# Second attention's scores without block-diagonal keys, and TensorE matmuls whose results nobody reads

## The chip, the cores and the metric

The kernel runs on one core of a Trainium2 chip. The metric is the device time of one execution in microseconds, of which several executions give a median. TensorE (PE) multiplies matrices, VectorE (DVE), ScalarE (ACT) and GpSimd (POOL) work on rows of up to 128 partitions, and SyncE (SP) issues transfers (DMAs). Each engine runs its own list of instructions in order; semaphores join them.

## The reference, cut to what matters

```python
x = x + window_attention(group_norm(x))     # 16 images of 16x16 tokens, 128 channels; 16 heads of 32
t = to_tokens(x)
t = t + attn(ln(t))                         # the second attention: 8 heads of 16
t = t + moe(ln(t))                          # 8 experts, top 2 of them for each token

def attn(x):                                # one image: 256 tokens, 128 channels
    qkv = x @ w_qkv + b_qkv
    q, k, v = heads_of_16(qkv)
    attn = softmax(einsum('bhqd,bhkd->bhqk', q, k) * c ** -0.5)
    return einsum('bhqk,bhkd->bhqd', attn, v) @ w_out + b_out
```

The second attention's scores are, for each of the 8 heads, a product of 256 queries and 256 keys over 16 channels. The kernel splits queries and keys into a high part rounded to the type fp32r and the remainder as a low part, and sums the four products of the parts.

## The kernel before, in words

All 16 images are software-pipelined. An iteration i works on up to eight images at once, each in another stage, and each engine goes through eight steps n = 0 to 7 in an order written out by hand. The stages are X (group norm, image i+2), G (queries, keys and values of the first attention, i+1), A (windowed first attention, i), M (its output projection, layer norm, and the projections of the second attention, i-1), Bm (the second attention, one head per step n, i-2), R (its output projection, i-3), L (router logits; the image's `slots` in DRAM are cleared, i-4) and K (each token's place in its experts' lists, and four indirect scatters of token rows on GpSimd at n = 6, i-5). Iterations 0 to 1 are the ramp, 16 to 20 the drain. An image's period here runs from one head 0 of Bm to the next. Four periods come before the first scatters; the ten after them hold scatters, and then the drain begins. After the drain the routing tables are finished, 39 tiles of 256 rows go through the experts (L1365 to L1393), and the two rows of each token are added.

The second attention before the change: at n = 5 of M, ScalarE writes the keys' high part (L646) and VectorE the low part (L929) into `kst1`. SyncE waits for the low part (`m_klo`) and copies the 16 rows of each head with one DMA into `kbd1` (L433, eight for an image). `kbd1` holds four blocks of 256 columns for each of two groups of heads, a head's block being zero outside its 16 rows, so that a matmul over all 128 rows of `q1` sees one head alone. GpSimd clears the two buffers once (L505). At n = 6 ScalarE (L675) and VectorE (L903) write `q1` likewise. In an iteration's step n, head n of Bm takes four matmuls with 256 moving columns (L1180), which at n = 0 wait for the queries' low part and for the eight DMAs (L1174), and on every odd step for the first attention's adds. They write `pSB` on even and `pSA` on odd steps. Then, at n = 0 and n = 4, come the windowed scores of A in 32x64 tiles (L1199) into `pSA` and `pTA`. VectorE takes the rows' maxima (L938), ScalarE the exponentials (L704), VectorE the reciprocals of their sums (L838), GpSimd multiplies (L548), and two steps later TensorE transposes (L1211); four heads at a time it multiplies by the values (L1227, 128x32 tiles). GpSimd's list also holds the first attention's multiply (L556) in front of the transposes L1296, and the scatters (L582).

SyncE's list for an iteration is: the next image's tokens `xt` (L413), the 1 MB of zeros into `slots` (L419), the residual (L424), which waits for R at n = 5, and the eight key copies (L433). Split products are three matmuls each, L1139 to L1141; L1286 is the first attention's output projection.

## Time and profile before

| | us |
|---|---|
| median of 3 runs | 817.3 |
| lowest, highest | 813.43, 821.74 |
| the profiled execution's own time | 815.25 |
| its span in the profile | 813.4 |
| mean granted TensorE clock over the span | 0.899 |

The durations used are those of the profiled execution, so a sum over them stands against 815.25 us, which is 2.05 us below the median of the three runs; the span leaves 1.85 us outside it. A granted clock of 1.00 is 2.4 GHz, one of 0.50 is 1.2 GHz; a mean between them says how much of a stretch stood at either.

### The profile page before, as it was taken

Reading aid. Unit: us, or ns where it says so; the run is one execution under the profiler, and the core shown is the slowest. Engines: PE = TensorE matmul, PEld = TensorE weight load, DVE = VectorE, ACT = ScalarE, POOL = GpSimd, SP = SyncE. Lnnn points to the kernel's source line nnn. Section 1 sums busy time; section 2 is a strip of 40 time slices with the busy share of each in tenths; the row PEclk is TensorE's granted clock in tenths of the full one; section 3 lists DMA queues with packets and bytes.
Section 4 is the critical chain, followed back from the end, with each engine's and each line's share of the span. In section 5 each row is a group of like instructions: output and inputs, shape, how many; then the busy total and the mean of one; then the engine's idle time right before and its main releaser. Section 6 shows DMA issues by size and latency. Waiting matters only on the chain. (4 is left out here: it accounts for less than half of the span.)

```text
span 813.4 us, 19815 instructions
## 1 busy us (share of the span) xinstructions
PE 636.2 (78%) x6838; PEld 536.7 (66%) x6838; DVE 513.5 (63%) x1513; ACT 509.5 (63%) x1427; POOL 479.3 (59%) x556
## 2 busy tenths in 40 slices
PE   2777898998999988898888998878753299998920
PEld 2556787776777767677777777756542187887810
DVE  5665767777778687777867778674332355564522
ACT  3555878787777688777877777655540166665600
POOL 6354556557675766867667575674554335655645
PEclk9698999999999899999999999897785599999965
DMA  7002203123041321404314041230732212222248
GB/s 206 14 2 34 32 5 93 21 75 90 18 107 19 89 49 59 105 9 100 60 48 103 12 99 27 81 81 25 197 126 78 66 54 79 83 83 68 79 120 219
DMA packets 54218, 59.25 MB, mean 73 GB/s; under 512 B 10371, under 2 KB 49411, under 8 KB 53603
## 3 DMA queue, kind: packets, MB, share of 16 engines
q1 hardware_dynamic: 44918, 45.65, 22.3%
q0 software_dynamic: 4544, 9.38, 3.2%
q10 hardware_dynamic: 4656, 2.95, 1.3%
q8 instruction: 56, 0.92, 0.5%
q14 instruction: 44, 0.35, 0.1%
HBM read 36.00 MB, written 28.64 MB: 79 GB/s over the span
## 5 line engine op out<-in xcount | busy, mean ns | idle before, releaser
L548 POOL TENSOR_TENSOR pb<-pb,rcb 128x512 f32<-128x512 f32 x128 | 155.5, 1215 | 177.2 <-DVE rcb L838 176.5
L593 POOL DMA_INDIRECT ysl<-yo,dst x78 | 74.7, 957 | 68.6 <-issue 33.5
L704 ACT ACTIVATE pb<-pSB,mxb 128x256 f32<-128x256 f32 x128 | 59.5, 469 | 58.9 <-DVE mxb L938 58.4
L1211 PE MATMUL pTB<-ident,pb 128*128 128x128 f32 x512 | 86.5, 296 | 12.1 <-ACT ptb L718 8.0
L556 POOL TENSOR_TENSOR pa<-pa,rca 128x512 f32<-128x512 f32 x64 | 67.2, 1051 | 29.0 <-DVE rca L1003 29.0
L718 ACT ACTIVATE ptb<-pTB 128x512 f32<-128x512 f32 x128 | 77.0, 602 | 6.0 <-PE pTB L1211 5.2
L704 ACT ACTIVATE pb<-pSA,mxb 128x256 f32<-128x256 f32 x128 | 59.7, 475 | 32.2 <-DVE mxb L938 25.8
L582 POOL DMA_INDIRECT slots<-rec,slot x64 | 63.2, 988 | 18.5 <-issue 17.2
L1211 PEld LDWEIGHTS pTB<-ident,pb 128*128 128x128 f32 x512 | 62.9, 150 | 16.5 <-issue 10.7
L938 DVE TENSOR_REDUCE mxb<-pSB 128x2 f32<-128x512 f32 x64 | 43.9, 686 | 41.4 <-PE pSB L1180 21.5
L724 ACT ACTIVATE pta<-pTA 128x512 f32<-128x512 f32 x64 | 38.4, 599 | 44.3 <-PE pTA L1296 44.1
L1180 PE MATMUL pSB<-kbd,q 128*128 128x256 f32 x256 | 47.6, 310 | 13.4 <-issue 11.6
L1296 PE MATMUL pTA<-ident,pa 128*128 128x128 f32 x256 | 43.6, 298 | 14.0 <-POOL pa L556 8.3
L1086 DVE COPY xs<-pG 128x256 f32<-128x256 f32 x39 | 16.6, 425 | 59.0 <-PE pG L1365 33.6
L1180 PEld LDWEIGHTS pSB<-kbd,q 128*128 128x128 f32 x256 | 37.5, 200 | 21.7 <-issue 19.3
L1139 PE MATMUL pG<-xnh,w0h 128*128 128x256 f32 x120 | 42.8, 357 | 11.2 <-POOL xnl L570 5.5
L1180 PE MATMUL pSA<-kbd,q 128*128 128x256 f32 x256 | 50.9, 325 | 0.0
L938 DVE TENSOR_REDUCE mxb<-pSA 128x2 f32<-128x512 f32 x64 | 43.9, 686 | 10.7 <-PE pSA L1180 9.6
L1271 PE MATMUL pOA<-pta,v 128*64 128x64 f32 x1024 | 45.9, 234 | 6.1 <-ACT t2f L686 3.6
L993 DVE TENSOR_REDUCE sma<-pa 128x8 f32<-128x512 f32 x64 | 43.6, 681 | 10.9 <-ACT pa L694 10.3
L1199 PE MATMUL pTA<-k,q 32*64 32x64 f32 x1024 | 43.6, 229 | 8.6 <-issue 8.6
L1271 PEld LDWEIGHTS pOA<-pta,v 128*64 128x64 f32 x1024 | 37.3, 143 | 17.8 <-issue 13.7
(213 smaller groups left out, 1955.3 us busy)
## 6 DMA issues: line engine op xcount, KB each, us to landing
slots<-sel_dram SPq DMA_DIRECT2D x16, 1040.0 KB
kbd<-kst SPq DMA_DIRECT2D x128, 64.0 KB
xt<-slots SPq DMA_DIRECT2D x39, 130.0 KB
xch<-x_ch_dram SPq DMA_DIRECT2D x4, 512.0 KB, 6.8
xt<-x_tok_dram SPq DMA_DIRECT2D x16, 128.0 KB
xch<-t SPq DMA_DIRECT2D x16, 128.0 KB, 2.0
fw<-f_dram SPq DMA_DIRECT2D x1, 2048.0 KB, 9.1
yc<-ysl SPq DMA_DIRECT2D x8, 256.0 KB, 9.3
```

Of the source, the lines that this page charges most:

```text
L548: pool.tensor_tensor(pb[:, b, :, :], pb[:, b, :, :], rcb[:, b, :].unsqueeze(2).to_broadcast([128, 2, TOK]), ALU.mult).then_inc(sb_nrm, 1)
L556: pool.tensor_tensor(pa[:, u, :, :], pa[:, u, :, :], rca[:, b, :].unsqueeze(2).to_broadcast([128, 8, WIN]), ALU.mult).then_inc(sa_nrm, 1)
L582: pool.indirect_dma_start(slots, bass.IndirectOffsetOnAxis(ap=slot[:, K.par, k, s:s + 1], axis=0), rec[:, K.par, s, k, :], None).then_inc( ...
L593: pool.indirect_dma_start(ysl, bass.IndirectOffsetOnAxis(ap=dst[:, t % YB, n:n + 1], axis=0), yo[:, t % YB, n, :], None).then_inc(y_dma[t ...
L704: last = a.activation(pb[:, b, qc, :], (pSB, pSA)[n % 2][:, qc * TOK:(qc + 1) * TOK], ACT.Exp, bias=mxb[:, b, qc:qc + 1], accum_out=smb[:, ...
L718: a.activation(ptb[:, (J.j * BU + k) % PTBUFS, :, :], pTB[:, :].rearrange("p (a b) -> p a b", a=2), ACT.Copy).then_inc(tb_ev, 1)
L938: v.tensor_reduce(mxb[:, b1, :], bank[:, :].rearrange("p (a k) -> p a k", a=2), AX.X, ALU.max, negate=True).then_inc(sb_max, 1)
L993: v.tensor_reduce(sma[:, b, :], pa[:, u, :, :], AX.X, ALU.add).then_inc(sa_sum, 1)
L1180: mm = pe.matmul((pSB, pSA)[n % 2][:, qc * TOK:(qc + 1) * TOK], q1[:, Bm.par, n // 4, qc * 128:(qc + 1) * 128], kbd1[Bm.par][:, part, n // ...
L1199: mm = pe.matmul(bank[WIN * w:WIN * w + WIN, (pr * NCH + c) * WIN:(pr * NCH + c + 1) * WIN], q0[D0 * r:D0 * r + D0, A.par, c, t:t + WIN], ...
L1211: mm = pe.transpose(pTB[:, kc * TOK + qc * 128:kc * TOK + (qc + 1) * 128], pb[:, k % PBUFS, qc, kc * 128:(kc + 1) * 128], ident[:, :])
L1271: mm = pe.matmul(pOA[WIN * jj:WIN * jj + WIN, w * WIN:(w + 1) * WIN], v0[:, J.par, w, jj, u, :, :].rearrange("p a d -> p (a d)"), pta[:, u ...
```

## The change

Keys: `kst1`, `kbd1`, the eight DMAs of each image (128 in all), the two clears and the waits on them are gone. The columns of the second attention's query and key weights are permuted on the chip into `w1p`, so that the 16 channels that the weights held for the high part of a head and the 16 for its low part come out in 32 adjacent rows. Queries: ScalarE multiplies by `is_low`, which is 0 or 1 for each row, with a bias `bq1l` to match; VectorE's part now spans 128 rows and not 64. Keys are written straight into `k1` and read from there. A head's four matmuls read rows 32*(n % 4) to 32*(n % 4) + 31 of `q1` and `k1`; their number and their 256 columns are as before.

Setup: the biases `bq1` and `bk1` are loaded with 16 small DMAs where there were 2, ahead of `bv1s`, `rws` and `rbs` on SyncE; ScalarE has four strided copies of 128 x 128 and one of 256 columns where it had one scaling of 256 columns; VectorE gets two small operations.

Unread matmuls: `keep_awake(bank, count)` issues matmuls of 128x128 by 512 columns of `w0h` into a bank that is free at that point. There are 6 ahead of the first image's projections; 1 a step in iteration 1; 3 (`AWAKE`) ahead of the scores of steps 0 and 4 in each of 14 iterations, behind waits for VectorE's adds and ScalarE's evictions that free `pTA`, waits which before stood only behind the head's own scores; 12 and 2 ahead of transposes of image 0; 2 a step in iterations 15 (but step 0) and 16; and 4 a step in 17 and 18. Another 32, of 128 columns in full fp32, stand between the last product of the routing tables and the experts' first tile.

```diff
-            sp.dma_start(bq1s[:, :], bq1).then_inc(d_c1, 16)
-            sp.dma_start(bk1s[:, :], bk1).then_inc(d_c1, 16)
+            for r in range(4):
+                for t in range(2):
+                    rows, of_head = slice(PAD1 * r + D1 * t, PAD1 * r + D1 * t + D1), slice(64 * t + D1 * r, 64 * t + D1 * r + D1)
+                    sp.dma_start(bq1s[rows, :], bq1[of_head, :]).then_inc(d_c1, 16)
+                    sp.dma_start(bk1s[rows, :], bk1[of_head, :]).then_inc(d_c1, 16)
...
-                    for h in range(8):
-                        rows = slice(D1 * h, D1 * h + D1)
-                        sp.dma_start(kbd1[M.par][rows, :, :, h % 4, :].bitcast(f32), kst1[rows, :, :, :].bitcast(f32))\
-                          .then_inc(k1_dma[M.par], 16)
...
-                        wait(a, k1_dma[(M.par + 1) % 2],
-                             (M.half + M.par) * 128 if M.j > 0 else 0)
+                        wait(a, sb_mm, (M.j - 1) * BU)
...
                             last = a.activation(q1[:, M.par, g, :], pM[:, g * TOK:(g + 1) * TOK], ACT.Identity,
-                                                bias=bq1x[:, g:g + 1])
+                                                scale=is_low[:, 0:1], bias=bq1l[:, g:g + 1])
...
-                    a.activation(w1s[:, 0:QK1], w1s[:, 0:QK1], ACT.Copy, scale=SCALE1).then_inc(c_w1s, 1)
+                    for k in range(2):
+                        for t in range(2):
+                            a.activation(w1p[:, k * QK1:(k + 1) * QK1].rearrange("p (g r t d) -> p g r t d", g=2, t=2, d=D1)
+                                         [:, :, :, t, :],
+                                         w1s[:, k * QK1:(k + 1) * QK1].rearrange("p (g t r d) -> p g t r d", g=2, t=2, d=D1)
+                                         [:, :, t, :, :], ACT.Copy, scale=(SCALE1, 1.0)[k])
+                    a.activation(w1p[:, 2 * QK1:], w1s[:, 2 * QK1:], ACT.Copy).then_inc(c_w1s, 1)
...
+            def keep_awake(bank, count):
+
+                for _ in range(count):
+                    pe.matmul(bank[:, :], w0h[:, 0:128], w0h[:, 0:512], start=True, stop=True)
...
+                    if A is not None and M is not None and Bm is None:
+                        keep_awake(pSB, 1)
+                    if Bm is not None and A is not None and n % 4 == 0:
+                        wait(pe, sa_add, A.j * AU + n // 2)
+                        wait(pe, ta_ev, A.j * AU + n // 2 - 1)
+                        keep_awake(pTA, AWAKE)
+                    if G is None and Bm is not None and M is not None:
+                        if n > 0 or A is None:
+                            pe.wait_ge(g_ev, B * GU)
+                            keep_awake(pG, 2)
+                    elif A is None and R is not None:
+                        keep_awake(pG, 4)
                     if Bm is not None:
...
-                            pe.wait_ge(k1_dma[Bm.par], Bm.half * 128 + 128)
...
+                        r, g = PAD1 * (n % 4), n // 4
                         for qc in range(2):
                             for part in range(2):
                                 mm = pe.matmul((pSB, pSA)[n % 2][:, qc * TOK:(qc + 1) * TOK],
-                                               q1[:, Bm.par, n // 4, qc * 128:(qc + 1) * 128],
-                                               kbd1[Bm.par][:, part, n // 4, n % 4, :],
+                                               q1[r:r + PAD1, Bm.par, g, qc * 128:(qc + 1) * 128],
+                                               k1[r:r + PAD1, Bm.par, part, g, :],
                                                start=(part == 0), stop=(part == 1))
...
+            for _ in range(GATHER_AWAKE):
+                pe.matmul(pOB[:, 0:128], ones[:, :], later[:, :], start=True, stop=True)
             turn_tokens(0)
```

SyncE's instructions in two steady iterations, before: each iteration's key copies stand between its residual (`xch<-t2`) and the next tokens.

```order
L413 DMA xt<-x_tok_dram 128x2x128
L419 DMA slots<-sel_dram 8x4x8320
L424 DMA xch<-t2 128x256
L433 DMA kbd1_0<-kst1 16x4x256 x8
L413 DMA xt<-x_tok_dram 128x2x128
L419 DMA slots<-sel_dram 8x4x8320
L424 DMA xch<-t2 128x256
```

The same of the changed kernel: the next tokens and the zeros follow the residual directly, so they are issued as soon as that is, and no longer behind the wait for the keys' low part.

```order
L419 DMA xt<-x_tok_dram 128x2x128
L425 DMA slots<-sel_dram 8x4x8320
L430 DMA xch<-t2 128x256
L419 DMA xt<-x_tok_dram 128x2x128
L425 DMA slots<-sel_dram 8x4x8320
L430 DMA xch<-t2 128x256
L419 DMA xt<-x_tok_dram 128x2x128
```

TensorE from the end of an iteration's step 7 to the first tiles of A in the next, before: the value product of G, head 0's scores, then A.

```order
L1211 MATMUL pTB<-ident,pb 128x128 x4
L1271 MATMUL pOA<-pta,v0 64x64 x8
L1139 MATMUL pG<-wvh,xnh 128x512
L1140 MATMUL pG<-wvh,xnl 128x512
L1141 MATMUL pG<-wvl,xnh 128x512
L1180 MATMUL pSB<-kbd1_0,q1 128x256 x4
L1199 MATMUL pSA<-k0,q0 64x64 x2
L1199 MATMUL pTA<-k0,q0 64x64 x2
```

The same of the changed kernel: three unread matmuls into `pTA` have come in ahead of head 0's scores, which read `k1`.

```order
L1295 MATMUL pOA<-pta,v0 64x64 x8
L1143 MATMUL pG<-wvh,xnh 128x512
L1144 MATMUL pG<-wvh,xnl 128x512
L1145 MATMUL pG<-wvl,xnh 128x512
L1151 MATMUL pTA<-w0h 128x512 x3
L1204 MATMUL pSB<-k1,q1 128x256 x4
L1223 MATMUL pSA<-k0,q0 64x64 x2
L1223 MATMUL pTA<-k0,q0 64x64 x2
```

TensorE at the end of the drain, before: the last output projection, router logits and places, the last product of the routing tables (`total`), and the experts' first transposes (`xt2`).

```order
L1350 MATMUL pM<-ahead,ones 128x16
L1227 MATMUL pOB<-ptb,v1 32x256 x8
L1242 MATMUL pOA<-wo1s,o1 128x128 x4
L1310 MATMUL pOA<-ident,tn2 128x128 x2
L1336 MATMUL pM<-rws,t2f 128x8 x2
L1348 MATMUL pM<-both,later 128x16
L1350 MATMUL pM<-ahead,ones 128x16
L1348 MATMUL pM<-both,later 128x16
L1350 MATMUL pM<-ahead,ones 128x16
L1358 MATMUL pM<-total,ones 128x8
L1365 MATMUL pG<-ident,xt2 128x128 x2
```

The same of the changed kernel: unread matmuls between the steps' short products, and 32 behind the product of `total`.

```order
L1266 MATMUL pOA<-wo1s,o1 128x128 x4
L1151 MATMUL pG<-w0h 128x512 x8
L1336 MATMUL pOA<-ident,tn2 128x128 x2
L1151 MATMUL pG<-w0h 128x512 x4
L1362 MATMUL pM<-rws,t2f 128x8 x2
L1374 MATMUL pM<-both,later 128x16
L1376 MATMUL pM<-ahead,ones 128x16
L1374 MATMUL pM<-both,later 128x16
L1376 MATMUL pM<-ahead,ones 128x16
L1384 MATMUL pM<-total,ones 128x8
L1423 MATMUL pOB<-later,ones 128x128 x32
L1391 MATMUL pG<-ident,xt2 128x128 x2
```

## Rows read from the trace of the kernel before

**Rows 1.** The page: busy time and share of the engines.
```profile
PE 636.2 (78%) x6838; PEld 536.7 (66%) x6838; DVE 513.5 (63%) x1513; ACT 509.5 (63%) x1427; POOL 479.3 (59%) x556
```

**Rows 2.** The waits: engine line waited for: us in all, times, longest.
```profile
POOL pb L548 <- DVE rcb L838: 176.5, 102, 5.6
PE pSB L1180 <- issue: 11.6, 14, 3.0
```

**Rows 3.** Windows: length, busy us (x) of PE, PEld, DVE, ACT, POOL, clock, DMA.
```profile
134.00:166.00 32.00, 28.48 (x384) 24.13 (x384) 25.30 (x68) 25.23 (x78) 17.83 (x20) 1.00 0.20 50
305.00:339.00 34.00, 28.91 (x388) 24.70 (x389) 26.23 (x74) 26.38 (x80) 23.72 (x29) 1.00 0.27 70
198.33:545.56 347.23, 302.95 (x3850) 258.11 (x3851) 261.75 (x738) 257.18 (x773) 232.85 (x275) 0.95 0.25 63
551.00:562.00 11.00, 11.00 (x73) 8.95 (x72) 2.33 (x10) 4.45 (x14) 3.54 (x5) 0.54 0.03 8
578.10:591.70 13.60, 10.97 (x57) 9.14 (x57) 3.65 (x14) 5.97 (x19) 7.03 (x10) 0.50 0.94 283
```

**Rows 4.** The timeline of TensorE: back-to-back matmuls.
```profile
213.64 0.28 PE L1141 MATMUL pG<-xnl,w0h 128*128 128x256 f32 x1
213.76 0.38 PE L1211 MATMUL pTB<-ident,pb 128*128 128x128 f32 x2
...
286.38 0.39 PE L1140 MATMUL pG<-wvh,xnl 128*128 128x512 f32 x1
286.61 0.39 PE L1141 MATMUL pG<-wvl,xnh 128*128 128x512 f32 x1
...
297.05 0.28 PE L1141 MATMUL pG<-xnl,w0h 128*128 128x256 f32 x1
297.26 0.42 PE L1227 MATMUL pOB<-ptb,v 128*32 128x256 f32 x4
```

**Rows 5.** The timeline of an image with scatters, by engine.
```profile
297.09 5.10 SPq L433 DMA_DIRECT2D kbd<-kst  x8
...
304.87 0.70 PE L1180 MATMUL pSB<-kbd,q 128*128 128x256 f32 x4 [0.88 <-issue]
...
307.20 0.69 DVE L938 TENSOR_REDUCE mxb<-pSB 128x2 f32<-128x512 f32 x1 [2.67 <-remote]
...
305.39 0.96 POOL L582 DMA_INDIRECT slots<-rec,slot  x1 [0.30 <-issue]
...
307.37 1.04 POOL L556 TENSOR_TENSOR pa<-pa,rca 128x512 f32<-128x512 f32 x1
```

**Rows 6.** The timeline of TensorE: head 0 of the first and the fourth image.
```profile
71.40 0.71 PE L1180 MATMUL pSB<-kbd,q 128*128 128x256 f32 x4 [1.79 <-DMA kbd<-kst]
...
166.32 0.72 PE L1180 MATMUL pSB<-kbd,q 128*128 128x256 f32 x4 [0.63 <-issue]
```

**Rows 7.** The setup: SyncE and ScalarE.
```profile
2.16 6.39 SPq L388 DMA_DIRECT2D posr<-pos_dram  x16
...
18.00 0.43 SPq L405 DMA_DIRECT2D rbs<-rb_dram  x1
...
22.49 0.42 ACT L730 ACTIVATE q<-q 128x256 f32<-128x256 f32 x1 [0.29 <-DMA rbs<-rb_dram]
```

**Rows 8.** The chain that ended last, 540 to 660 us: start, us, what.
```profile
558.70 3.12 PE pM L1286 x16
577.00 3.02 issue
...
646.65 2.05 PE pSA L1372 x4
...
654.10 0.86 PE pSA L1372 x4
```

**Rows 9.** The timeline of TensorE: a warm out-projection, the first expert tile.
```profile
487.72 2.05 PE L1286 MATMUL pM<-wo0s,o 128*128 128x128 f32 x16
...
645.28 0.69 PE L1365 MATMUL pG<-ident,xt 128*128 128x128 f32 x2 [9.58 <-DMA xt<-slots]
```

46 lines of the change are left out of this document (27 added, 19 removed).

## The prediction

> **What bounds the kernel now.** I read the page's shares first, then the waits, then windows of single images, then the timeline around head 0, and last the chain that ended last. No engine is full: PE is the busiest with 78% of the span [rows 1]. In an image without scatters PE is busy for 28.5 of 32.0 us, in one with scatters for 28.9 of 34.0 us, at the full clock in both [rows 3]. So a steady image is some 29 us of PE work and 3.5 to 5 us of gaps, while GpSimd has slack: most of its idle time goes to waits for VectorE's reciprocals [rows 2]. PE's order, with the loop scores, maximum, exponential, reciprocal, multiply, transposes laid over it, sets the period, and what is added to PE lands on the path unless it falls into one of these gaps.
>
> Two places in a period are not PE's work. At head 0 PE stands for the key copies: SyncE needs 5.10 us to issue the eight of them [rows 5], and the idle time before the head's first matmul was 1.79 us in the first image and 0.63 us in the fourth [rows 6]; over the four periods without scatters the four of them sum to 5.2 us. In an image with scatters PE waited 0.88 us for it, and the head's scores, begun at 304.87, reached VectorE only at 307.20, after 2.67 us idle [rows 5]; without scatters the four matmuls take 0.72 us [rows 6]. So some 1.6 us more go there, with the key copies and the scatters (last one at 305.39) in flight together.
>
> The drain is another thing: there PE stood 3.02 us for the last image's copies, and its clock is low: 0.54 in 551 to 562 us and 0.50 in 578 to 592 us [rows 3, 8]. The same 16 matmuls take 3.12 us there and 2.05 us warm [rows 8, 9].
>
> **The change, part by part.** The sum is made against the profiled execution's 815.25 us, 2.05 us under the median of the runs shown.
>
> *Setup.* SyncE gets 14 more DMAs ahead of `rbs`. Sixteen small ones took 6.39 us, 0.40 each [rows 7], so `rbs` comes 5.6 us later; ScalarE's first scaling waits for exactly that DMA [rows 7] and everything in its list stands behind it, then VectorE's low part and the projections of image 0. Then ScalarE has five copies instead of one of 0.42 us: four of half the columns and one like it, some 1.5 us instead of 0.42, so +1.1. Together +6.7. The two clears of `kbd1` leave GpSimd's list, which has time then. The unread matmuls of the ramp keep the clock up for image 0's steps; I take 1.2 us for that (bounds 0 and 2.5), an estimate from what one fall costs below. **Ramp +5.5.**
>
> *Scores in 32 rows.* The count and the 256 columns are the same, so the matmuls cost the same; the trace has no 32-row matmul with 128 stationary columns, so I bound what surrounds it. A full-array product followed by another starts 0.12 us after it, followed by a 128x32-tile product 0.21 us after it [rows 4]: 0.09 us for going into another tile shape, and I take the same for coming out. Six heads pay both, the two that A's tiles follow only one: 6 x 0.18 + 2 x 0.09 = 1.26 us an image. Bounds: 0 (if rows alone are not such a shape) and 2.5 (if each costs double). The Trainium skill, in TensorEngine Tiling (Array Packing), on tiling modes, says that a change of mode drains the array; the rows agree that a change costs something, and the sum by either is this one.
>
> *Unread matmuls in the steady state.* 512 columns take 0.23 us at the full clock [rows 4]: six an image are 1.38 us. With the switches that is 2.64 us. PE's gaps (3.5 us an image [rows 3]) hide a part, mainly at step 4, where the evictions of the value product are waited for: I count 2.3 on the path. The waits ahead of them are for things that A's tiles two places on wait for anyway; behind them are head 0's and head 4's scores, and through these VectorE's maximum. Bounds: 0 and 2.64.
>
> *Four periods without scatters:* 4 x 2.3 = 9.2, less the 5.2 us of key waits. **+4.0.**
>
> *Ten periods with scatters:* of the 2.64 us, 0.78 (three unread matmuls and one switch) stand at step 0, where the stall was; the rest is 1.86, of which I take 1.3 on the path. At step 0, without the 0.88 us and the 1.6 us, GpSimd is next: after the last scatter (305.39) come two multiplies, the second of which, for A, starts at 307.37 and takes 1.04 us [rows 5], and step 1's transposes of `pa` need it. The step can come at most 1.0 us sooner. Net +0.3 an image. **+3.** The earlier `xt` and zeros on SyncE (they no longer queue behind the key copies) go to buffers that are waited for an image later, and take no time; if the 1 MB now meets the scatters, that is the second rival.
>
> *Clock in the steady state.* 198.33 to 545.56 us are ten periods at a mean clock of 0.95 [rows 3], that is 34 us at 1.2 GHz. Ten undisturbed ones would be 340 us, so the falls cost 7.2 us. They begin just after step 0, where PE stands idle and then runs A's 32x64 tiles. The change removes the idle time and puts three full-array products there, but makes eight sets of scores narrow. I take three quarters of it back, **-5.4** (bounds -7.2 and +9).
>
> *Drain.* The wait of 3.02 us goes, but for the queries' low part and the switch: -2.5. At 1.2 GHz PE pieces take half as long again [rows 8, 9]; the two windows of 11.0 and 13.6 us hold 22 us of busy PE [rows 3], a third of which is 7.3; the unread matmuls should save most, less what they add themselves to the short steps: -6. The first expert tile has 2.05 us where later ones have 0.86 [rows 8], and 32 unread matmuls stand ahead of it: -1.5. They are full fp32 of 128 columns; eight such products are the 16 pieces of 2.05 us warm or 3.12 us cold [rows 8, 9], so 32 are 8.2 to 12.5 us, where PE idled 9.58 us before the tile's first transposes [rows 9]. If the clock doesn't rise in them, they end 3 us late. **-10** (bounds -13 and +1).
>
> The sum: 5.5 + 4.0 + 3.0 - 5.4 - 10.0 = -2.9, which is 812.3 us.
>
> **The rivals.**
> 1. *PE isn't what binds.* If switches and unread matmuls fall into gaps, two thirds of the 9.2 + 13 us counted for them vanish: about 797 us. For it: 3.5 to 5 us of gaps in every period [rows 3]. Against: the gaps are waits inside the loop, and a later matmul moves them along.
> 2. *The stall at step 0 stays.* The label on VectorE's wait names no releaser [rows 5], so the key copies need not be the cause: GpSimd's scatters with the zeros and tokens that now come earlier would do as well. Then the 1.0 us of ten periods is not gained: 812 + 10 = 822 us. The zeros may then also hold up the scatters by themselves.
> 3. *The clock falls more often,* the slower side. In 551 to 562 us PE was busy for the whole 11.00 us at a clock of 0.54, and in 134 to 166 us for 89% of it at 1.00 [rows 3], so it isn't busy time that keeps the clock, but what is done. If scores of 32 rows keep it up worse than those of 128, and six unread matmuls an image don't make up for it, the falls double: +7.2 in place of -5.4, and 4 us of the drain's gain go: 829 us. It decides from about fourteen falls in the steady state, where there are eight stretches now.
> 4. *Weight loads come into the open.* All four matmuls of a head now use the same 32 rows. If each load then waits for the matmul ahead of it, that is at least one more spacing of 0.12 us for each [rows 4], 32 an image: 3.8 x 15 = 58 us, about 870 us. Against it: products that use the same (all) rows follow each other after 0.12 us with a load between them [rows 4]. The Trainium skill, in TensorE: Matmul & The Clock Gate, Part 3, says that loads overlap matmuls in flight only when the row group differs; by that rule this rival would happen, and before's rows speak against it.
>
> **How the numbers follow.** The forecast (0.44) is 812 us, by itself 802 to 820. Rival 1 has 0.20, rival 2 0.21, rival 3 0.12, rival 4 0.03. The range 797 to 829 leaves out half of rivals 1 and 3 and all of 4, a little under two in ten. A measurement can tell about 1%, here 809.1 to 825.5. Faster by over 1%: 0.17 of the forecast, 0.19 of rival 1: 0.36. Slower: 0.08 of rival 2, 0.10 of rival 3, and rival 4: 0.21. Within: 0.43.
>
> **What would show it.** After the change, head 0's first row should have no idle time from keys; VectorE's maximum at step 0 should wait under 1 us in a period with scatters, with GpSimd running from the first scatter to A's multiply without idle (else rival 2). Full-array products should start 0.09 us later next to scores than before (rivals 1 and 4: nothing, or 0.12 more per matmul). The windows of ten periods should have a clock of 0.98 or more (rival 3: 0.91). A's first tiles should come 5 to 6 us later, and the last product of head 7's drain some 8 us nearer to the start of its image. The prediction would be most wrong if the ramp's 14 DMAs were hidden, or the clock went the other way.

## The result

The changed kernel takes 871.28 us (median of 4 runs, 864.54 to 873.86) against 818.16 us for the kernel before beside it (median of 4): a ratio of 1.061 (1.057 to 1.066), slower. The profiled execution's span is 862.7 us against 813.4 us. The forecast was 812 us, within 797 to 829.

Head 0 of Bm marks the periods in both traces. The first scatters' period begins at 198.3 us before and 201.4 us after; the fifteenth image's head 0 comes at 545.6 and 608.9 us; the ends are the spans. So the 49.3 us come from three pieces:

| | before | after | difference | forecast |
|---|---|---|---|---|
| start to the first period with scatters | 198.3 | 201.4 | +3.1 | +9.5 |
| the ten periods with scatters | 347.2 | 407.5 | +60.3 | -2.4 |
| from there to the end | 267.8 | 253.8 | -14.0 | -10.0 |

Head 0 stands in the spans, so these are pieces of the two profiled executions, of which the changed kernel's was the fastest of its four. What made the change slower lies in the ten periods.

The page of the changed kernel, first the engines' shares, as in [rows 1], then the granted clock of TensorE in 40 slices:

```profile
PE 740.3 (86%) x7112; PEld 598.8 (69%) x7112; DVE 503.7 (58%) x1515; ACT 516.8 (60%) x1431; POOL 472.1 (55%) x554
...
PEclk9799999999969696979788887978999789999975
```

PE is busier by 104 us, though only some 57 us of unread matmuls were added (210 of 512 columns at 0.23 us and the 32, 9 us): the same instructions last longer. The clock row shows 6 to 8 in most slices from the twelfth to the twenty-eighth, where the periods with scatters lie. The waits, as in [rows 2]:

```profile
POOL pb L541 <- DVE rcb L836: 230.1, 96, 6.5
...
DVE mxb L936 <- remote: 25.3, 9, 2.8
```

GpSimd waits longer for the reciprocals, since the whole loop is longer; and VectorE's wait for head 0, labelled remote, is still there (nine times, up to 2.8 us), though the key copies are gone. The wait of PE for key copies is no longer among its rows. Windows, columns as in [rows 3]: one period without scatters, one with, and the ten together:

```profile
134.50:167.70 33.20, 31.32 (x392) 25.54 (x391) 25.15 (x69) 26.47 (x80) 18.64 (x21) 1.00 0.11 42
319.60:360.60 41.00, 38.00 (x395) 30.89 (x394) 25.57 (x74) 26.81 (x79) 23.64 (x29) 0.83 0.11 41
201.40:608.90 407.50, 378.52 (x3924) 303.80 (x3923) 255.29 (x737) 262.65 (x775) 234.14 (x276) 0.84 0.11 41
```

Without scatters the period is 33.2 us where it was 32.0 [rows 3], at the full clock. With them it is 41.0 us at a mean of 0.83, and eight periods in a row are 41.0 to 41.2 us. In all but the first of the ten a low stretch begins some 4 us after head 0 and lasts 13.65 us; the tenth has another of 6.8 us, and the first only one of 3.4 us. One period, cut at the two places (columns as above, the clock third from the end): ahead of the fall TensorE is busy for 3.04 of 4.10 us, in it for 13.18 of 13.65.

```profile
360.63:364.73 4.10, 3.04 (x76) 2.75 (x75) 1.50 (x3) 3.09 (x10) 3.77 (x6) 1.00 0.12 37
364.73:378.38 13.65, 13.18 (x75) 10.29 (x74) 6.05 (x18) 6.17 (x19) 7.43 (x10) 0.50 0.00 1
378.38:401.61 23.23, 21.81 (x248) 17.85 (x247) 18.02 (x54) 17.55 (x52) 12.46 (x14) 1.00 0.17 65
```

TensorE's timeline at the end of that fall, and at the next head 0:

```profile
372.19 1.22 PE L1204 MATMUL pSB<-k,q 32*128 32x256 f32 x4
...
376.88 2.77 PE L1310 MATMUL pM<-wo0s,o 128*128 128x128 f32 x16
379.50 0.60 PE L1322 MATMUL pTA<-ident,pa 128*128 128x128 f32 x4
380.03 0.74 PE L1204 MATMUL pSA<-k,q 32*128 32x256 f32 x4
380.70 0.39 PE L1143 MATMUL pG<-xnh,w0h 128*128 128x256 f32 x1
...
400.84 0.84 PE L1151 MATMUL pTA<-w0h 128*128 128x512 f32 x3
401.61 0.73 PE L1204 MATMUL pSB<-k,q 32*128 32x256 f32 x4
```

The four scores of head 2 (372.19) last 1.22 us, the out-projection 2.77 us where 2.05 is warm [rows 9], and behind it everything is back: the scores at 380.03 take 0.74 us. So the clock rises in the out-projection that follows head 2, and not before it. The last two rows show the price of the three unread matmuls (0.77 us from the first of them to the scores, at the full clock) and that the four narrow scores take 0.73 us, where four over 128 rows took 0.70 to 0.72 [rows 5, 6]: their weight loads are as hidden as before. GpSimd and VectorE around the same head 0:

```profile
398.41 1.07 POOL L575 DMA_INDIRECT slots<-rec,slot  x1 [0.17 <-issue]
...
402.31 0.96 POOL L575 DMA_INDIRECT slots<-rec,slot  x1 [0.30 <-issue]
...
404.29 1.06 POOL L549 TENSOR_TENSOR pa<-pa,rca 128x512 f32<-128x512 f32 x1
...
404.16 0.69 DVE L936 TENSOR_REDUCE mxb<-pSB 128x2 f32<-128x512 f32 x1 [2.82 <-remote]
```

The scores' rows end at 401.61 + 0.73 = 402.34, but VectorE can read them only at 404.16, 1.8 us later. This is the stall of [rows 5], 2.82 us idle where it was 2.67, with no key copy in flight.

### The profile page after: what moved, and what is told of

Read it like the earlier page. It is cut to its first block and busy times, and to the rows that moved or that the text cites. A ratio compares the mean times of both kernels' runs of the same rounds, so it can differ in the third digit from the quotient of the medians.

```text
span 862.7 us, 20278 instructions
## 1 busy us (share of the span) xinstructions
PE 740.3 (86%) x7112; PEld 598.8 (69%) x7112; DVE 503.7 (58%) x1515; ACT 516.8 (60%) x1431; POOL 472.1 (55%) x554
## 5 line engine op out<-in xcount | busy, mean ns | idle before, releaser
L1235 PE MATMUL pTB<-ident,pb 128*128 128x128 f32 x512 | 90.2, 304 | 4.4 <-ACT ptb L710 2.5
L716 ACT ACTIVATE pta<-pTA 128x512 f32<-128x512 f32 x64 | 38.2, 597 | 77.0 <-PE pTA L1322 77.0
L1143 PE MATMUL pG<-xnh,w0h 128*128 128x256 f32 x120 | 48.7, 406 | 4.9 <-ACT v L655 2.8
L1204 PE MATMUL pSB<-k,q 32*128 32x256 f32 x256 | 51.7, 325 | 0.0
L1204 PE MATMUL pSA<-k,q 32*128 32x256 f32 x256 | 51.6, 324 | 0.0
L1295 PE MATMUL pOA<-pta,v 128*64 128x64 f32 x1024 | 48.2, 242 | 2.6 <-ACT pta L716 1.1
L1295 PEld LDWEIGHTS pOA<-pta,v 128*64 128x64 f32 x1024 | 39.4, 150 | 15.0 <-issue 11.3
L1223 PE MATMUL pSA<-k,q 32*64 32x64 f32 x1024 | 41.0, 222 | 10.0 <-issue 10.0
L1204 PEld LDWEIGHTS pSB<-k,q 32*128 32x128 f32 x256 | 37.8, 204 | 15.6 <-issue 14.2
L1204 PEld LDWEIGHTS pSA<-k,q 32*128 32x128 f32 x256 | 37.6, 203 | 15.1 <-issue 15.1
L747 ACT ACTIVATE ws<-fw 128x773 f32 x39 | 33.0, 848 | 25.0 <-DVE t_exp L1052 18.2
```

Source lines behind the costliest of these rows:

```text
L1143: pe.matmul(out_, wh, xh, start=True, stop=False)
L1204: mm = pe.matmul((pSB, pSA)[n % 2][:, qc * TOK:(qc + 1) * TOK], q1[r:r + PAD1, Bm.par, g, qc * 128:(qc + 1) * 128], k1[r:r + PAD1, Bm.par, ...
L1235: mm = pe.transpose(pTB[:, kc * TOK + qc * 128:kc * TOK + (qc + 1) * 128], pb[:, k % PBUFS, qc, kc * 128:(kc + 1) * 128], ident[:, :])
L1295: mm = pe.matmul(pOA[WIN * jj:WIN * jj + WIN, w * WIN:(w + 1) * WIN], v0[:, J.par, w, jj, u, :, :].rearrange("p a d -> p (a d)"), pta[:, u ...
```

## The experiments

The runs came to four chips, each time with the kernel before beside them, and the ratios are against that. First chip (kernel before 794 us): e1 to e4. Second (822 us): c1, c2, e5, e6. Third (821 to 823 us): c3, e7, e8, e9, e14, e15. Fourth (828 us): e10 to e13. Times of different chips are not compared, only ratios and what the periods look like. In the last column are the ten periods from the fifth head 0 to the fifteenth, with their mean clock, in the profiled execution. Other numbers in the scores (e1, e5, e7, e12, e14, e15) mean that the kernel no longer computes the reference; its instructions stay the same.

| | edit | median us | ratio (95%) | ten periods: us, clock |
|---|---|---|---|---|
| e1 | scores over 128 rows, first chip | 794.6 | 1.000 (0.997 to 1.003) | 339.3, 0.97 |
| e2 | scatters behind the pipeline | 866.4 | 1.090 (1.081 to 1.098) | 346.0, 0.97 |
| e3 | no steady unread matmuls | 834.6 | 1.050 (1.043 to 1.058) | 384.7, 0.85 |
| e4 | before, with the unread matmuls of the ends | 785.8 | 0.990 (0.983 to 0.997) | 336.0, 0.97 |
| c1 | the changed kernel, second chip | 869.5 | 1.061 (1.055 to 1.068) | 407.5, 0.84 |
| c2 | the kernel before, second chip | 822.3 | 1.000 (0.996 to 1.003) | 355.1, 0.92 |
| e5 | scores over 64 rows | 865.0 | 1.057 (1.051 to 1.063) | 406.6, 0.84 |
| e6 | 12 unread matmuls for 3 | 879.1 | 1.073 (1.067 to 1.080) | 396.6, 0.94 |
| e7 | scores over 128 rows, third chip | 808.0 | 0.983 (0.977 to 0.989) | 351.8, 0.96 |
| c3 | the changed kernel, third chip | 866.5 | 1.053 (1.045 to 1.060) | 405.0, 0.84 |
| e8 | scatters at step 7 | 842.9 | 1.023 (1.018 to 1.029) | 375.5, 0.94 |
| e9 | as e4, third chip | 811.8 | 0.987 (0.981 to 0.993) | 349.5, 0.95 |
| e10 | 1 unread at each step | 878.6 | 1.065 (1.055 to 1.076) | 402.2, 0.86 |
| e11 | 2 unread at each step | 917.9 | 1.105 (1.090 to 1.119) | 434.6, 0.82 |
| e12 | two bias DMAs | 881.1 | 1.063 (1.053 to 1.073) | 412.1, 0.83 |
| e13 | e4 and the scatters at step 7 | 832.8 | 1.005 (1.000 to 1.009) | 368.0, 0.93 |
| e14 | 128 rows at steps 0 to 2 | 814.5 | 0.992 (0.988 to 0.996) | 354.6, 0.96 |
| e15 | 128 rows at steps 3 to 7 | 846.3 | 1.033 (1.024 to 1.041) | 375.6, 0.90 |

### The width of the scores: e1, e7, c3, e5

```diff
-                                               q1[r:r + PAD1, Bm.par, g, qc * 128:(qc + 1) * 128],
-                                               k1[r:r + PAD1, Bm.par, part, g, :],
+                                               q1[:, Bm.par, g, qc * 128:(qc + 1) * 128],
+                                               k1[:, Bm.par, part, g, :],
```

> The changed kernel with one difference: the second attention's scores read all 128 rows of q1 and k1 in place of a head's 32, so a score is the sum over four heads (the softmax and all behind it computes on other numbers). Count, columns, waits and unread matmuls are those of the changed kernel. After the change a period with scatters takes 41.0 us with 13.65 us of it at half clock. Theory A (the narrow scores are what lets the clock fall): periods of 34 to 35 us, mean clock over the ten periods at least 0.97, time 800 to 812 us. Theory B (the stall during the scatters, not the width of the scores, lets the clock fall): periods stay near 41 us, time 865 to 875 us. Theory C (leaving and entering narrow tiles costs): periods some 1.2 us shorter, clock as it is.

The ten periods were 33.4 to 35.0 us, and the ratio 1.000, as theory A (the narrow scores let the clock fall) has it. But this first chip had something else: head 0 came without the stall. TensorE's and VectorE's rows of e1 in a period with scatters:

```profile
231.42 0.63 PE L1204 MATMUL pSB<-k,q 128*128 128x256 f32 x4
...
232.08 0.69 DVE L936 TENSOR_REDUCE mxb<-pSB 128x2 f32<-128x512 f32 x1 [0.80 <-PE pSB L1204]
```

The scores end at 231.42 + 0.63 = 232.05 and VectorE reads at 232.08. So e1 had neither the narrow scores nor the stall, and it could not tell which of the two absences mattered. The changed kernel had to be seen again, and e1 repeated where the stall is.

> The changed kernel itself once more, since the kernel before took 794 us here against 817 us where it was first compared, and TensorE's lag during the scatters (1.6 to 2.3 us a period there, before and after) was absent in the profiles of the first four experiments. Theory A (narrow scores let the clock fall, whatever the stall): periods with scatters of 38 to 41 us, ratio 1.05 to 1.07. Theory B (the stall tips it): without the stall no falls, periods of 34 us, ratio 0.98 to 1.00.

> The kernel before itself once more, for a profile beside the others. No lag during the scatters, periods with scatters of some 33.5 us against 34.8 where it was first profiled, ratio 1.00.

This second chip had the stall in both kernels, against what I had expected of c2, and the kernel before had periods of 34.6 to 37.1 us; c1 repeats the 41.0 us and the 1.061. It left the question where it was, so both went to a third chip together:

> The changed kernel with scores over all 128 rows again (a sum over four heads; the softmax and all behind it computes on other numbers), because the first time it ran where TensorE shows no lag during the scatters, and the changed kernel itself was seen only where it does (periods of 41.0 us, ratio 1.061; with 64 rows the same). If the width alone decides: periods of 34 to 36 us and a ratio of 0.97 to 1.01 with the lag too. If the lag alone decides: 41 us and 1.06 with the lag, wherever the scores are read from.

> The changed kernel beside it. With the lag during the scatters: 41.0 us a period and 1.061, as twice. Without the lag: if the width alone decides, 38 to 41 us and 1.05 or more; if lag and width are both needed, 34 us and 0.98 to 1.00.

That chip has the stall: in nine of c3's ten periods and in six of e7's, VectorE reads head 0's scores 1.7 to 2.2 us after their end. Windows of e7: a stretch as long as a period, with scatters and at the full clock, and the ten periods:

```profile
230.00:264.00 34.00, 30.09 (x394) 25.93 (x394) 25.66 (x75) 26.47 (x79) 23.50 (x28) 1.00 0.13 49
196.10:547.90 351.80, 314.18 (x3924) 271.42 (x3923) 259.46 (x737) 259.75 (x774) 232.39 (x274) 0.96 0.13 47
```

The same ten of c3, beside it on the chip:

```profile
206.10:611.10 405.00, 376.74 (x3925) 301.94 (x3924) 255.19 (x737) 263.07 (x775) 232.58 (x274) 0.84 0.11 41
```

The same instructions (3924 and 3925 matmuls), waits, unread matmuls and scatters take 351.8 us over 128 rows and 405.0 us over 32; the whole kernel 808.0 and 866.5 us. With the stall present in both, the width alone decides: theory A. That e7 computes on other numbers doesn't explain it, since e5 below does so too and keeps the falls. In e7 the falls last 3.4 us each and come in seven of the ten periods.

> The changed kernel with scores read from 64 rows of q1 and k1 (two heads summed; the softmax and all behind it computes on other numbers). Theory A, by how much of the array a score fills: between 32 rows and 128 rows, so falls in some periods with scatters, periods of 34 to 38 us, 800 to 835 us. If only the tile mode mattered, it would be as the changed kernel with 32 rows.

My expectation was wrong: 64 rows are no middle. Eight of its ten periods are 40.9 to 41.2 us with 13.65 us at half clock, as with 32 rows.

### Which scores: e14, e15

```diff
+                        rows = slice(0, 128) if n < 3 else slice(r, r + PAD1)      # e14;  e15: n > 2
...
-                                               q1[r:r + PAD1, Bm.par, g, qc * 128:(qc + 1) * 128],
-                                               k1[r:r + PAD1, Bm.par, part, g, :],
+                                               q1[rows, Bm.par, g, qc * 128:(qc + 1) * 128],
+                                               k1[rows, Bm.par, part, g, :],
```

> The changed kernel with scores over all 128 rows at steps 0, 1 and 2 and narrow ones at steps 3 to 7 (the heads of the wide steps are sums over four heads; all behind computes on other numbers). If the heads in the thin stretch keep the clock down: falls of 3.4 us or none, 34 to 36 us a period, 0.98 to 1.01. If it is the period as a whole: 37 to 41 us.

> The reverse: narrow at steps 0, 1 and 2, all 128 rows at steps 3 to 7 (again other numbers). If the thin stretch decides: 40 to 41 us a period with 13.65 us at half clock, 1.05 to 1.06. If the period as a whole does: 35 to 38 us, since five of eight heads are wide.

The ten periods of e14, and then of e15:

```profile
199.90:554.50 354.60, 328.09 (x3924) 271.27 (x3923) 258.62 (x737) 261.11 (x774) 232.52 (x274) 0.96 0.13 46
```

```profile
204.10:579.70 375.60, 340.87 (x3924) 286.68 (x3923) 257.64 (x737) 260.29 (x775) 231.51 (x274) 0.90 0.12 44
```

Both ran on the chip of e7 and c3. Three wide heads of eight bring 405.0 us to 354.6, the five others bring it to 375.6 only. In e14 a period has 3.4 us at half clock, once 6.8 and twice none; in e15 four have 13.65 to 17.1 us (40.1 to 42.3 us a period) and three none (33.6 to 34.1 us). So no long fall came with wide heads at steps 0 to 2. Narrow ones there bring them, but not in every period as long as the other five are wide: of the six falls behind head 0 in e15 four last 13.65 us and two 3.4 us. I had expected e15 at 40 to 41 us a period throughout; the mean is 37.6 us, within what I had written down for the other theory, that the period as a whole decides. Both parts count, the first three heads more.

### Unread matmuls: e3, e6, e10, e11

```diff
-AWAKE = 3
+AWAKE = 0        # e3;  e6: 12
...
+                        if A is not None:                                  # e10, with AWAKE = 0; e11: 2
+                            keep_awake((pSB, pSA)[n % 2], 1)
```

> The changed kernel with AWAKE = 0: no unread matmuls ahead of the scores of steps 0 and 4, those of ramp, drain and the gap stay. Theory A and B alike: they are 1.38 us a period at the full clock and some 2 at half; if they do not hold the clock up at all, the periods become 1.5 to 2 us shorter, 20 to 25 us in all, 845 us. If they hold it up somewhat, the falls start to come in the periods without scatters too and the time is 870 to 885 us.

> The changed kernel with 12 unread matmuls ahead of the scores of steps 0 and 4 in place of 3: 18 more a period at 0.23 us, 4.1 us of TensorE at the full clock. By theory A they put activity in the thin stretch but at one place only: the falls end in most periods, which are then 34 + 4 = 38 us, 845 us in all; if the falls start two steps later, where there are none of them, the periods are 42 to 45 us and the time 890 us.

> The changed kernel with one unread matmul ahead of the scores of each of the eight steps, into the score bank, in place of three at steps 0 and 4: 8 x 0.23 = 1.8 us a period at the full clock against 1.4. If it is the distribution of full-array work over the period: the falls are fewer or shorter, 36 to 39 us a period, 825 to 850 us. If no full-array work mends it: 41 us, 870 us.

> The same with two at each step, 3.7 us a period at the full clock; e6 spent 5.5 us at steps 0 and 4 and had periods of 37.8 to 40.8 us. By the distribution: few falls left, 36 to 37 us a period (34 and the added work), 825 to 835 us. Else 42 us, 880 us.

What they cost was as counted: the third and fourth period are 31.8 and 32.4 us without (e3), 33.2 and 33.7 with six, and 37.3 us in the third with 24 (e6), 0.23 us each. e3 ran where there is no stall, and of its ten periods with scatters five are 38.1 or 38.2 us with 10.2 us at half clock, four 39.6 to 41.4 us, and one, without a fall, 32.4 us: without steady unread matmuls narrow scores let the clock fall without the stall too. No run of the changed kernel stands beside it on that chip, so what six of them are worth is not measured.

e6 has 37.8 or 37.9 us in three periods and 40.8 us in six. It runs beside c1 and shows both sides. Its falls behind head 0 are gone; what is left are falls of 6.8 us that begin some 26 us after it, 48 us at half clock in the ten periods where c1 has 133:

```profile
223.49:620.05 396.56, 376.61 (x4096) 303.04 (x4095) 258.55 (x737) 262.56 (x771) 231.20 (x273) 0.94 0.11 41
205.59:613.04 407.45, 378.70 (x3924) 303.45 (x3923) 255.31 (x737) 262.26 (x775) 234.07 (x276) 0.84 0.11 41
```

The first row is e6, the second c1: the ten periods get 10.9 us shorter. But the four ahead of them, which had little to win, get 18.0 us longer, so the whole is slower. Of my two guesses (845 and 890 us) neither came. e10 alternates at first, as two windows of neighbouring periods show:

```profile
247.60:281.70 34.10, 32.52 (x397) 26.16 (x396) 25.91 (x75) 26.27 (x80) 22.32 (x27) 1.00 0.12 46
281.70:326.10 44.40, 41.94 (x397) 32.95 (x396) 25.35 (x74) 27.16 (x80) 24.89 (x30) 0.77 0.11 39
```

34.1 us at the full clock, then 44.4 us at 0.77 with 20.5 us at half. So a period with narrow scores, unread matmuls and scatters does fit into 34 us, and all the rest is the fall. Sixteen spread ones (e11) made it worse: one period without a fall, 36.6 us, then eight of 44.2 to 44.4 us with 17.1 us at half. That goes against my idea that full-array work spread over the period mends it; at half clock each unread matmul costs 0.43 us, and they lengthen the stretch that they were to end.

### The stall during the scatters: e2, e8, e13

```diff
-                    if n == 6 and K is not None:      # e8; e13 the same on the kernel before
+                    if n == 7 and K is not None:
                         for s in range(2):
                             for k in range(2):
                                 pool.indirect_dma_start(
```

> The changed kernel, but all 64 scatters are issued behind the pipeline, out of records and slots kept for all 16 images; the result is the same. In the changed kernel TensorE's signals come up to 1.8 us late from the first scatter on, in each period. Theory A (narrow scores alone let the clock fall): the lag goes, but the clock still falls in most periods, 38 to 40 us each. Theory B (the scatters' stall tips it): no lag, no falls, periods of 33 to 34 us, as in the three without scatters. The scatters themselves then stand behind the pipeline, 64 x 1.26 = 80 us less what overlapped; so the total would be 862.7 - 10 x 7.5 + 60 to 80 = 850 to 870 us by B and 880 to 900 by A; the periods decide, not the total.

> The changed kernel with the four scatters of an image one step later in GpSimd's list, behind the multiplies and record copies of step 7. If TensorE's lag comes from the scatters, it moves with them: none at the last value product and head 0, some 1.7 us between steps 0 and 1. Then the thin stretch of step 0 is longer by it, and the falls start there: 41 to 43 us a period. If the lag belongs to step 7's own work, it stays where it was. If a period's length is set by GpSimd there, the four scatters (5.0 us) in front of head 0's multiply show as 2 to 3 us more.

> The kernel before with the unread matmuls of ramp, drain and gap, and the scatters behind step 7's multiplies. On the changed kernel that move gave 24 us (866.5 to 842.9), since the lag no longer met step 0's thin stretch. With block-diagonal keys there are only 7 to 10 us of falls in the steady state to win, and the multiply of head 0 comes behind the scatters: 0.98 to 1.00 of the kernel before, best guess 0.985, no better than without the move (0.987).

e2, on the first chip, where no stall was to be seen anyway, has the scatters behind the pipeline (records and slots kept for 16 images, and no waits for their reuse). Its ten periods:

```profile
205.10:551.10 346.00, 326.00 (x3925) 262.96 (x3924) 258.13 (x737) 260.48 (x776) 192.51 (x234) 0.97 0.11 40
```

Six of them are 33.7 to 33.8 us at the full clock, and none has a fall behind head 0, with narrow scores and six unread matmuls. The total doesn't gain, since the 64 scatters then stand by themselves. That is theory B's number, but e3 beside it fell without any stall, and the changed kernel itself was not run on that chip. So e2 shows that narrow scores hold the clock where nothing is scattered, as they do in most of the first four periods everywhere; by itself it doesn't show that the stall is what tips them.

The periods of the other runs tell more, since the stall doesn't come in all of them. In c3 the first of the ten has its last scatter end at 204.95 and its head 0 at 206.08; VectorE reads 0.04 us after the scores. In the next one the last scatter runs from 240.53, behind head 0 at 239.83. VectorE's reads of the two heads, and the two periods:

```profile
206.85 0.69 DVE L936 TENSOR_REDUCE mxb<-pSB 128x2 f32<-128x512 f32 x1 [1.06 <-PE pSB L1204]
...
242.36 0.69 DVE L936 TENSOR_REDUCE mxb<-pSB 128x2 f32<-128x512 f32 x1 [2.83 <-remote]
```

```profile
206.08:239.83 33.75, 31.82 (x396) 26.03 (x395) 25.83 (x74) 26.38 (x79) 21.93 (x27) 1.00 0.12 45
239.83:280.89 41.06, 38.07 (x396) 30.92 (x395) 25.56 (x74) 26.84 (x79) 23.74 (x29) 0.83 0.11 41
```

Without the stall the changed kernel's period holds the clock, with it there is the fall. The two neighbours of e10 above differ in the same way (VectorE reads 0.04 and 1.86 us after head 0's scores); in the 4.1 us from their head 0 on TensorE is busy for 3.61 us without the stall and for 2.86 us with it. Over the seven profiles with narrow (or 64-row) heads at step 0, six to eight unread matmuls an image and the scatters at step 6 (the changed kernel, c1, c3, e5, e10, e12, e15), 59 periods have a lag of 1.7 us or more at head 0. All 59 have a fall within 5 us of it, 55 of them one of 13.65 us or more. Of the 11 periods with a lag of 0.6 us or less two have one, 3.4 us in the changed kernel and 13.65 us in e15. e6, whose 12 unread matmuls ahead of head 0 let the scatters end before head 0's scores do, has no lag there and no fall. The stall comes ahead of the fall in time. With wide scores it doesn't decide: of e7's six periods with the lag four have no fall there. So with the unread matmuls the long falls take both, narrow scores and the stall, with that one exception in e15; without them (e3) narrow scores are enough. This is read off periods that came out one way or the other; the run that moves the scatters alone is e8, and it agrees.

e8 shows whose stall it is. Rows of TensorE, VectorE and GpSimd, in that order, from one period of e8:

```profile
245.80 0.73 PE L1204 MATMUL pSB<-k,q 32*128 32x256 f32 x4
...
252.61 0.37 PE L1376 MATMUL pM<-ahead,ones 128*128 128x16 f32 x2
...
246.57 0.69 DVE L936 TENSOR_REDUCE mxb<-pSB 128x2 f32<-128x512 f32 x1 [1.07 <-PE pSB L1204]
...
254.25 0.17 DVE L846 TENSOR_TENSOR lg<-pM,rbs 128x16 f32<-128x16 f32 x1 [1.78 <-PE pM L1376]
...
248.42 1.08 POOL L575 DMA_INDIRECT slots<-rec,slot  x1 [0.17 <-issue]
...
254.33 1.04 POOL L541 TENSOR_TENSOR pb<-pb,rcb 128x512 f32<-128x512 f32 x1
```

With the scatters beginning at 248.42, head 0's scores end at 246.53 and are read at 246.57, no lag; but the places' product ends at 252.61 + 0.37 = 252.98 and VectorE sees it at 254.25, 1.3 us late. The lag has moved with the scatters, as expected of it, and is not that of the key copies or of step 7's work. I had expected longer falls from it, 41 to 43 us a period; they got shorter. The kernel gains 24 us (866.5 to 842.9, c3 beside it): two periods have 10.2 us at half clock, one 6.8 and seven at most 3.4. GpSimd is the new bound there: head 0's multiply starts at 254.33, behind the scatters, and the seven periods are 35.0 to 37.2 us, not 34. e13 has this price where there were no long falls to win: 1.005, where I had guessed 0.985. It has falls of its own, too: nine of its ten periods have 3.4 or 6.8 us at half clock. It stands on another chip than e4 and e9, so the size of the difference is not measured.

### The setup and the ends: e12, e4, e9

```diff
-            for r in range(4):
...
+            sp.dma_start(bq1s[:, :], bq1).then_inc(d_c1, 16)
+            sp.dma_start(bk1s[:, :], bk1).then_inc(d_c1, 16)
```

> The changed kernel with the two biases loaded by one DMA each, as before the change (they then lie in other rows, so queries and keys get other biases; nothing else differs): 14 DMAs less. If they stand on the path as forecast, the first head 0 comes 5.6 us sooner and so does the end, 864 us against 869.5. If the setup hides them, 0 to 2 us.

SyncE and ScalarE in the changed kernel, against [rows 7]:

```profile
24.04 0.43 SPq L411 DMA_DIRECT2D rbs<-rb_dram  x1
...
26.72 0.91 ACT L724 ACTIVATE w1p<-q 128x128 f32<-128x128 f32 x4 [3.99 <-DMA rbs<-rb_dram]
```

`rbs` is issued 6.0 us later (24.04 for 18.00), and ScalarE begins 4.2 us later, after 3.99 us idle. The same row in e12:

```profile
21.96 0.89 ACT L721 ACTIVATE w1p<-q 128x128 f32<-128x128 f32 x4
```

With two DMAs it begins at 21.96 and waits for nothing, and the first head 0 comes at 68.9 us, where the changed kernel's three profiles have 72.8, 73.9 and 74.4: 3.9 to 5.5 us. On e12's own chip e10 and e11, whose ramps are the changed kernel's, have it at 73.1 and 71.6, which is 4.2 and 2.7 us. The total shows none of it (1.063): in e12 falls also came in two early periods and in the first with scatters (10.2, 6.8 and 13.7 us at half clock). So a gain ahead of the pipeline doesn't show in the total; no run of the changed kernel on that chip says how much of it was lost to these falls.

The drain's part of the edit (the ramp's, and the 32 of the gap, are those of the change):

```diff
+                    if G is None and Bm is not None and M is not None:
+                        if n > 0 or A is None:
+                            pe.wait_ge(g_ev, B * GU)
+                            keep_awake(pG, 2)
+                    elif A is None and R is not None:
+                        keep_awake(pG, 4)
```

> The kernel before with only the unread matmuls of ramp, drain and the gap before the experts (6, 12, 2 and 1 in the ramp, 2 a step in iterations 15 and 16, 4 a step in 17 and 18, 32 before the experts); block-diagonal keys stay, nothing in the steady state is changed. After the change the stretch from head 0 of the fifteenth image to the end is 14 us shorter than before, of which 3 are the key copies' wait. So 805 to 810 us, some 10 us under the kernel before, if that gain was the clock; no change if it came from the keys and the order on SyncE.

> The kernel before with the unread matmuls of ramp, drain and the gap alone, once more: 0.990 (0.983 to 0.997) the first time. From the clock: the drain's two stretches and the first experts, 8 to 12 us where the lag is, so 0.985 to 0.990.

On two chips, 0.990 and 0.987, both intervals below 1: the unread matmuls of ramp, drain and gap are worth about 1% to the kernel before, with its block-diagonal keys and nothing added in the steady state. It is the fastest version here that computes the reference. The 32 ahead of the experts, and the tile's transposes behind them, in the changed kernel:

```profile
692.53 8.98 PE L1423 MATMUL pOB<-later,ones 128*128 128x128 f32 x64
702.25 0.44 PE L1391 MATMUL pG<-ident,xt 128*128 128x128 f32 x2 [0.74 <-DMA xt<-slots]
```

They take 8.98 us, and the transposes waited another 0.74 us for their tokens, so they cost nothing in this execution. The experts' first pieces in the chain that ended last:

```profile
706.31 1.10 PE pSB L1398 x4
707.41 0.86 PE pTB L1398 x4
```

1.10 and 0.86 us against 2.05 for the first piece of [rows 8].

## Why the prediction was wrong

**The step that failed is the clock in the steady state.** "The change removes the idle time and puts three full-array products there, but makes eight sets of scores narrow. I take three quarters of it back, -5.4 (bounds -7.2 and +9)." The first premise of that term failed: the idle time was not removed, since VectorE still waits 2.82 us at head 0 and TensorE is busy for only 3.04 of the 4.10 us ahead of the fall. The second half of the sentence was the effect, and the three full-array products did not outweigh it. In place of -5.4 us, and of the bound of +9, the falls cost some 59 us more, by an estimate from the periods: 407.5 us less ten times c3's undisturbed 33.75 us is 70, and before it was 347.2 us less ten times 33.6 us (the mean of the three undisturbed), 11. On one chip, width alone moved the ten periods by 53.2 us (351.8 to 405.0). Up to 10 us of these are the tile shapes (an estimate from the 0.9 and 1.1 us of a period below), the rest is the clock.

**Rival 3 was the mechanism, with a size far too small.** It let the falls double at the price that they had before: 7.2 us for 34 us at half clock, 0.2 us for each. Both factors were off. The time at half clock in the ten periods went from 34 to 133 us, since each fall lasts 13.65 us instead of mostly 3.4; and a microsecond at half clock costs about 0.5 (c3's 41.06 us less the 33.75 us of its undisturbed period, over 13.65 us). The forecast's 0.2 came in part from its baseline: it took 34.0 us for an undisturbed period, where the three of the kernel before are 34.1, 34.0 and 32.8 us; with their mean it would have been 0.3. That TensorE's gaps hid more of the short falls before is possible, but no run shows it.

**Rival 2 was right too, and is the other half of the cause:** the stall at step 0 stays, 2.82 us for 2.67. I had put it down to key copies and scatters together, because in before's trace it showed only where both were. It needs only the scatters (e8). So the 1.0 us of ten periods was not gained, and the stall that stayed is what the long falls come with (59 of 59 periods above).

**Rival 4's 870 us is a coincidence.** Four narrow scores take 0.73 us, loads hidden, as rows of the full array had said. The Trainium skill, in TensorE: Matmul & The Clock Gate, Part 3, says that weight loads overlap matmuls in flight only when the row group differs. These four use the same rows, and the trace doesn't agree: a load that had to wait would have made them longer than the 0.70 to 0.72 us of before. A total that fits shows no mechanism.

**Rival 1** is out: six unread matmuls lengthen a period by 1.3 to 1.4 us (e3), all of their 1.38 us.

**Tile shapes.** Forecast 1.26 us an image. Going into narrow scores takes 0.53 us from the transposes ahead where it took 0.36 before, coming out 0.67 where it was 0.56 (the rows at 379.50 to 380.70 above, and the same place before, at the end of this paragraph), so 0.28 us for a head with both, half as much again as the 0.18 counted. The third and the fourth period take 33.2 and 33.7 us in the changed kernel, 32.3 and 32.6 in e7: 0.9 and 1.1 us for the width, within the bounds. TensorE in step 3 of a full-clock period, before:

```profile
317.07 0.60 PE L1296 MATMUL pTA<-ident,pa 128*128 128x128 f32 x4
317.43 0.72 PE L1180 MATMUL pSA<-kbd,q 128*128 128x256 f32 x4
317.99 0.28 PE L1139 MATMUL pG<-xnh,w0h 128*128 128x256 f32 x1
```

Together with the unread matmuls and without the key waits, the four periods came to +1.7 us against a forecast of +4.0. The clock helped there, which the sum had not counted: the first two of them have 10.2 us at half clock before and none after, and are 0.9 and 0.4 us shorter, while the third and fourth, at the full clock in both kernels, are 1.2 and 1.7 us longer (forecast +1.0 each).

**Setup.** The DMAs' 5.6 us were 6.0 on SyncE and 2.7 to 5.5 at head 0. The first head 0 was only 1.4 us later in the profile, since it no longer waits 1.79 us for keys (which the sum had in the next term) and has less of the ramp at half clock (10.2 for 13.7 us). The two terms together were +3.1 where +9.5 was forecast.

**Drain and experts.** -14.0 us for -10, but not by the forecast's terms. From the fifteenth head 0 to the sixteenth it is -5.2 us (34.5 to 29.3, with 3.4 us for 12.2 at half clock), of which the 3.02 us of the key copies' wait are a part. From there to the experts' first tile it is only -1.2 us, though the mean clock went from 0.60 to 0.87. So up to that tile -6.4 us stand against -8.5. The experts, from the first tile's transposes to the last tile's, gave -7.9, where only the first tile was to gain 1.5 us. The two stretches before, then after:

```profile
580.02:645.28 65.26, 29.15 (x170) 23.15 (x171) 20.01 (x104) 17.66 (x53) 31.56 (x47) 0.60 0.36 124
645.28:771.20 125.92, 118.27 (x595) 100.36 (x596) 69.17 (x224) 77.78 (x149) 65.19 (x69) 0.97 0.26 77
```

```profile
638.17:702.28 64.11, 44.58 (x296) 34.93 (x295) 20.43 (x106) 18.30 (x55) 33.20 (x48) 0.87 0.25 82
702.28:820.30 118.02, 114.09 (x596) 98.00 (x597) 68.70 (x224) 76.37 (x148) 65.06 (x68) 1.00 0.29 82
```

The second chip has the same (129.3 us in c2, 118.7 in c1). The unread matmuls alone don't do it: on the third chip e9 has them and takes 127.1 us there, 3.4 of them at half clock, where c3 takes 118.1. What in the changed kernel makes the experts faster is open.

## What to carry to other kernels

Matmuls with the same columns and the same duration are not the same to TensorE's clock: before narrowing the contraction from 128 rows, look where in a period the clock already falls (here 3 to 5 us behind head 0) and what idles just ahead of it, and count the narrow scores there at the price of a much longer low stretch, not of one fall as it was. Unread matmuls pay where TensorE idles anyway (ramp, drain, gaps: 1% here). Where it is the engine that is short, 24 an image shortened the periods with falls (e6) and lengthened the others by more, and no number of them tried here made the narrow kernel as fast as the kernel before. And a stall that shows only where two things meet must not be charged to the one that is about to be removed; moving each by itself, as e8 does, takes one experiment.

## What the runs showed of the hardware that was not expected

- Scores over 64 rows behave as over 32 (eight periods of 40.9 to 41.2 us with 13.65 us at half clock each, 406.6 us for ten at 0.84), not as over 128 (351.8 us for ten, at 0.96).
- The low clock set in 4.1 to 4.5 us after head 0 and its stretch was 13.65 us long in nine periods in a row, in each of three executions of the changed kernel, on at least two chips.
- TensorE's completions reach VectorE up to 2.3 us late while GpSimd issues indirect scatters (1.8 us in the changed kernel, 1.3 us in e8, up to 2.3 us before), in the profiles of three of the four chips; in the four profiles of the first chip there was no such lag, and the kernel before took 794 us there against 818 to 828 us. What in the chip makes the lag is open.
- In the same kernel, a period with narrow scores and without that lag held the clock (33.75 us), and the next one with it fell (41.06 us).
- Why 128 rows at steps 0 to 2 shorten a fall and 16 unread products over 128 rows an image do not is open as well. The runs place the effect, they don't explain it.
